# Attention scores and side work as column quarters: 64x32 tiles in place of 64x128

## The reference

```python
x = x + 0.5 * ffn(layernorm(x), k0, k1, k2, s0, s1, s2)
x = x + attn(layernorm(x), wq, bq, wk, bk, wv, bv, wo, bo)   # 16 heads of 16 dims
x = x + 0.5 * ffn(layernorm(x), k0, k1, k2, s0, s1, s2)

# ffn: weights are +1 or -1 by a boolean; features 2*256 -> 1024 -> 1024 -> 256
h = concatenate([x, -x]); h = 2 * relu(s0 * (h @ w(k0)))
h = 2 * relu(s1 * (h @ w(k1))); return s2 * (h @ w(k2))
# attn
scores = softmax(q @ k.T / sqrt(16)); att = scores @ v; return att @ wo.T + bo
```

## Time and profile before

| | |
|---|---|
| median of 3 executions | 1523.57 us (1523.52 to 1525.18) |
| span of the profiled execution, first to last instruction | 1521.2 us |
| PE busy | 1512.4 us (99%), 12471 matmul records |
| ACT busy | 1129.3 us (74%), 8 to 9 tenths in the attention stretch |
| DVE busy | 574.2 us (38%) |
| chain of work that ended last | PE 99% |
| granted TensorE clock, mean | 0.999 |

### The profile page before, as it was taken

One profiled execution on the slowest core, in us unless ns is written; L12 is line 12 of the kernel. 1 busy time (PEld: TensorE's weight loads), 2 busy tenths in 40 slices (PEclk: granted clock), 3 DMA queues, 4 the chain that ended last, 5 costly groups with the idle time before them and its releaser, 6 DMA issues.

```text
span 1521.2 us, 31574 instructions
## 1 busy us (share of the span) xinstructions
PE 1512.4 (99%) x12471; PEld 606.1 (40%) x12471; DVE 574.2 (38%) x1298; ACT 1129.3 (74%) x1654; POOL 59.7 (4%) x65
## 2 busy tenths in 40 slices
PE   9999999999999999999999999999999999999999
PEld 5555455334334333333333334334333334334354
DVE  7645764511431243234332333242241332323462
ACT  3221222888889988898989989889988988988721
POOL 2010011001000100010100000000000000000000
PEclk9999999999999999999999999999999999999999
DMA  4122223212331231232223123111213212311110
GB/s 139 42 84 51 75 80 113 71 51 81 84 73 41 96 95 40 67 113 63 81 53 95 40 53 94 39 49 59 81 39 67 82 51 65 104 41 21 47 28 16
DMA packets 110139, 101.46 MB, mean 67 GB/s; under 512 B 55846, under 2 KB 95526, under 8 KB 109990
## 3 DMA queue, kind: packets, MB, share of 16 engines
q1 hardware_dynamic: 109158, 98.60, 23.0%
q10 hardware_dynamic: 832, 0.79, 0.2%
HBM read 61.87 MB, written 25.43 MB: 57 GB/s over the span
## 4 chain that ended last, share of the span: by engine, by line
PE 99%; DVE 0%; ACT 0%; issue 0%; POOL 0%; POOLq 0%
PE psum L888 31%; PE psum L850 30%; PE psum L872 16%; PE psum L750 12%; PE psum L762 3%; PE psum L738 3%; PE psum L769 2%; PE psum L782 1%; PE psum L688 0%; PE psum L775 0%; DVE xn L972 0%; DVE h_lo L982 0%; PE psum L710 0%; DVE x_sb L987 0%; ACT xn L911 0%
## 5 line engine op out<-in xcount | busy, mean ns | idle before, releaser
L942 ACT ACTIVATE prob<-psum 128x512 f32<-128x512 f32 (+1 forms) x1438 | 1016.6, 784 | 120.1 <-PE psum L872 115.4
L888 PE MATMUL psum<-prob,v_sb 128*17 128x512 f32 x4096 | 489.4, 595 | 0.0
L872 PE MATMUL psum<-q_st,k_st 64*128 64x512 f16 x2048 | 350.1, 379 | 0.2
L915 ACT ACTIVATE h_hi<-psum 128x512 f16<-128x512 f32 x183 | 109.6, 604 | 215.8 <-PE psum L750 164.6
L980 DVE TENSOR_SCALAR h_hi<-psum 128x512 f16<-128x512 f32 x73 | 50.5, 692 | 433.8 <-PE psum L850 433.8
L982 DVE SCALAR_TENSOR_TENSOR h_lo<-psum,h_hi 128x512 f16<-128x512 f32 x256 | 169.0, 688 | 86.9 <-ACT h_hi L915 84.4
L888 PEld LDWEIGHTS psum<-prob,v_sb 128*17 128x17 f32 x4096 | 95.3, 96 | 262.9 <-issue 166.4
L872 PEld LDWEIGHTS psum<-q_st,k_st 64*128 64x128 f16 x2048 | 82.5, 94 | 279.1 <-ACT prob L942 210.7
L850 PE MATMUL psum<-h_hi,w 64*128 64x512 f16 x1184 | 152.1, 376 | 0.2 <-ACT h_hi L915 0.2
L850 PE MATMUL psum<-h_lo,w 64*128 64x512 f16 x1184 | 152.0, 376 | 0.0
L750 PE MATMUL psum<-h_hi,w 128*128 128x512 f16 x432 | 102.5, 380 | 2.2 <-DVE h_lo L982 2.2
(11 more groups left out here) (109 smaller groups left out, 860.0 us busy)
## 6 DMA issues: line engine op xcount, KB each, us to landing
k_st<-k_halves SPq DMA_DIRECT2D x64, 512.0 KB, 4.4
q_halves<-piece SPq DMA_DIRECT2D x32, 256.0 KB, 2.5
q_st<-q_halves SPq DMA_DIRECT2D x64, 128.0 KB, 4.8
x_rows<-x_sb SPq DMA_DIRECT2D x16, 256.0 KB, 2.2
k_halves<-piece SPq DMA_DIRECT2D x16, 256.0 KB, 2.8
att_rows<-o_sb SPq DMA_DIRECT2D x128, 32.0 KB
x_sb<-x_rows SPq DMA_DIRECT2D x8, 512.0 KB, 4.0
att_t<-att_rows SPq DMA_DIRECT2D x16, 256.0 KB
```

Of the source, the lines that this page charges most:

```text
L872: mm = pe.matmul(psum[:, score_bank[h + r], :], k_st[rows, slot, t * P:(t + 1) * P], q_st[rows, slot, :], start=True, stop=True)
L888: mm = pe.matmul(psum[32 * j:32 * j + va, O_BANK, :], v_sb[:, b * key_tiles + t, GROUP * g4 + j, :], prob[:, h % PROBS, :], start=(t == 0) ...
L915: act.activation(hi, psum[:, bank, :], ACT.Relu).then_inc(act_done, 1)
L942: act.activation(prob[:, to:to + count, :], psum[:, bank:bank + count, :], ACT.Exp, scale=score_scale / QK_SCALE ** 2).then_inc(exp_sem, 1)
```

## The change

Every matmul of `pe_pair` and `pe_scores` becomes four, one for each quarter of its 128 columns: the quarter's 32 columns of the weights, the same moving operand, and the quarter's 32 partitions of the same bank. A pair of two matmuls of 64 rows by 128 columns becomes a group of eight of 64 rows by 32 columns: four quarters on one half of the rows, then four on the other. The semaphore is raised by the last quarter. Waits, banks, the list of steps and the instructions of all other engines stay as they are; only line numbers move. The products with v (line 888, now 893) stay at 128 rows by 32 columns.

```diff
+        QUARTERS = [slice(c, c + P // 4) for c in range(0, P, P // 4)]
+
         def pe_pair(s):
...
                 for bank, first in ((s, 0), (s.mate, 1)):
                     r, m = (first + turned + part) % 2, bank.m
                     rows, cols = slice(64 * r, 64 * r + 64), slice(m * P, (m + 1) * P)
-                    to = psum[:, bank.bank, :]
+                    wide = slice(0, BANK)
...
-                        to = psum[:, bank.bank, column * dim:(column + 1) * dim]
+                        wide = slice(column * dim, (column + 1) * dim)
                         w, a = src[rows, k, tile * P:(tile + 1) * P], wide_w[rows, k, :]
-                    mm = pe.matmul(to, w, a, start=(turned == 0 and j == 0), stop=(turned == 1 and j == length - 1))
+                    for c in QUARTERS:
+                        mm = pe.matmul(psum[c, bank.bank, wide], w[:, c], a,
+                                       start=(turned == 0 and j == 0), stop=(turned == 1 and j == length - 1))
                     if i == 2 * n - 1:
                         mm.then_inc(mm_done, 1)
...
             for r in range(2):
                 rows = slice(64 * r, 64 * r + 64)
-                mm = pe.matmul(psum[:, score_bank[h + r], :], k_st[rows, slot, t * P:(t + 1) * P], q_st[rows, slot, :],
-                               start=True, stop=True)
+                for c in QUARTERS:
+                    mm = pe.matmul(psum[c, score_bank[h + r], :], k_st[rows, slot, t * P:(t + 1) * P][:, c],
+                                   q_st[rows, slot, :], start=True, stop=True)
             mm.then_inc(qk_sem, 1)
```

## The result

The changed kernel takes 1609.84 us (median of 4 executions, 1606.12 to 1619.18) against 1523.57 before: a ratio of 1.0568, 95% interval 1.0551 to 1.0585. The forecast was 1528.7 with a range of 1475 to 1535. The direction was right, the size was not: 86 us were lost where 5 were expected.

The account below looks back on a forecast made before the run. PE, busy 99% of the span, was taken to bound the kernel. Span 1521.2 plus 5.1 for the lag of eight starts, other terms 0, gave 1526.3; with the median 2.4 above, 1528.7 us, range 1475 to 1535.

Parts of the forecast that it names:

- More instructions: On PE, 19,900 more matmuls and as many loads; the sequencer can issue one in 0.0068 us, so cost 0.
- rival 4: PE's instruction pages come late: 167 more, 1729 us if each is exposed, 1595 if a third; chance 0.05.
- Eight starts in place of two: Ahead of the v products, the group's last matmul starts 0.02 us later a step, costing 5.1 us in all.
- The shape change: Between scores and v products, changing rows alone still costs the 0.09 to 0.10 us gap; saving 0, bounds 0 and 49.
- Rival 1: The gap at the v products goes when columns agree, saving 49 us: 1475 us; chance 0.18.
- Four streams, loads: In PE's groups, four quarters' operand streams run at full rate and loads hide under running matmuls; each costs 0.
- rivals 2 and 3: On PE: starts or streams have a floor, 1591 to about 2260 us, chance 0.08; loads come late, about 1832, chance 0.05.
- Other engines: Outside PE nothing moves; exponentials start 0.02 us later with the scores, and ACT has room.
- The sum: Whole kernel: profiled span 1521.2 + 5.1 = 1526.3; the median stands 2.4 above its span, giving 1528.7 us.

Follow-up runs that it names:

- experiments 2: Changed kernel, but from the third group of heads on only 128 of 2048 columns of k are fetched: 1573.55 us, ratio 1.0340 against the kernel before.
- 3: Changed kernel with the next group's k sent in four parts, one a step over four steps, same bytes: 1576.39 us, ratio 1.0351 against the kernel before.
- 5: Changed kernel with each transfer of k followed by an equal one into device memory nobody reads: 1670.56 us, ratio 1.0952 against the kernel before.
- the two controls: Kernel before with each k transfer doubled: 1525.10 us, ratio 1.0004; kernel before with k cut to 128 columns from the third group: 1523.64 us, ratio 0.9997.
- 1: The change with column halves, 64 columns a tile, in place of quarters: 1529.16 us, ratio 1.0036 against the kernel before.
- Experiment 4: Changed kernel with the l3 work left as pairs of 64 rows by 128 columns, quarters elsewhere: 1572.27 us, ratio 1.0322 against the kernel before.
- after_small_k: The kernel of experiments 2: the change with k cut to 128 columns from the third group of heads on, 1573.55 us.
- run 64: Not a follow-up kernel: the stretch of 64 l3 matmuls in a row in the changed kernel's own trace, which takes 0.87 us.
- double-k run: The changed kernel with each transfer of k followed by an equal one into unused device memory: 1670.56 us, ratio 1.0952.

## Why the prediction was wrong, step by step

**The step that failed: pages, in "More instructions ... Cost 0" and in rival 4.** The part on instructions asked only whether PE's sequencer can issue one in 0.0068 us. It can, but it must have it first. Rival 4 did count the pages (167 more forecast, 155 came) and how often one is due ("one every 4.8 us of attention"), and then took the packet's own 1.2 us for the price of a page and wrote "Fetched ahead, as now, it is hidden", with a chance of 0.05. Two things were wrong. The time to compare with is not the packet's own: at the waits PE goes on 2.2 to 3.0 us after a packet's start, and the packet starts 1.2 us after PE has begun the page before at the median, 5.8 us at the worst, behind a group's k and q, in transfers of 512 KB that take 5.4 us to land. That is some 3.6 us as a rule and up to 8.5 (at 1140.47), against the 3.3 and 5.2 us that a page lasts. And "as now" held for a page every 13 us: the kernel before fetched 83 between 300 and 1400 us, so it had cover for all of this; the changed one fetched 231 between 300 and 1500, one every 5.2 us with the waits counted. The rival's own version with a third of the pages exposed, 1595, was nearest to the truth: 49 late steps for 155 added pages, at 86.9 / 49 = 1.8 us each and not 1.2. That is luck, as no row stood behind its third. The rival's sign, idle stretches of about a microsecond at regular counts of instructions, is what the trace shows: 57.0 / 44 = 1.3 us, at multiples of 256.

What shows the cause: at equal instructions the loss moves with the data beside the pages (experiments 2, 3 and 5, with nothing moved in the two controls), and at equal data with the instructions in a stretch (1 and 4). The waits stand at multiples of 256 instructions, and each ends behind a page's packet. That a page is asked for about one page ahead is worked out from the packets' times, not recorded. The 21 l3 steps that stay late without the k bursts fit this too: in the dense part of an l3 step a page lasts 2.2 us, less than the 1.2 + 2.4 us that a page needs at the median from the start of the page before. In `after_small_k` the l3 wait that ends at 819.30 had next to nothing else on the DMA engines: 1.4 us to the packet and 2.5 from there. No run took all other transfers away, so how much of the 33.1 us is left to them is open.

The Trainium skill, "Runtime: NRT & Kernel Launch", section "Instruction fetch mechanics", says that instructions come in blocks of 256 while the block before is executed, and that crossing into the next is mostly hidden because an engine issues more slowly than blocks arrive. The first half agrees with this trace: 256 instructions in a packet, and waits at multiples of 256. The second does not hold for this kernel: 57.0 us of waits, on the engine that bounds it.

**Eight starts in place of two: right.** Forecast 0.02 us a step; the median step is 0.019 longer. From the last score group's first start to its last it is 23 ns at the median of undisturbed steps (3 before), and from that last start to the first v product 306 ns in both kernels. All steps that are not late sum to 6.8 us against 5.1.

**The shape change: right, no gain.** 306 - 216 = 0.09 us, the same whether rows alone change or both. Rival 1 (1475 us) needed less than 0.07. Experiment 4 measured the third kind, columns alone at 64 rows: 0.09 to 0.12 at each of four places.

**Four streams, loads: right.** Groups of eight take 0.216 us, in l3 (656.24 - 655.37) / 8 = 0.109, the numbers of the prediction, over runs of 64 matmuls: 0.87 / 64 = 0.0136 us a start. That ends rivals 2 and 3. The Trainium skill's 25 ns as the least distance between matmul starts ("TensorE: Matmul & The Clock Gate", section "Wait — 56ns, not 53.3ns?"), which the prediction cited against the change, would by an estimate from that figure have made this run 64 x 0.025 = 1.6 us; the trace, with 0.87, does not agree.

**Other engines: right.** Busy times of DVE, ACT and POOL moved by less than 5 us.

**The sum.** Its 2.4 us are the median less the span of another execution. Within one execution they are 4.0 (1525.18 against 1521.2; 4.1 in the changed kernel). The forecast does not hang on it, as it comes to the median before plus 5.1 us.

## What to carry to other kernels

Cutting a matmul into column tiles multiplies instructions at equal work: count how long 256 of them last on the engine at its densest place, and compare that with how long a page takes to arrive, counted from the start of the page before (here some 3.6 us at the median, up to 8.5 behind the longest burst of data), not with what an instruction costs to issue. Where an engine stops at "issue" in the middle of work that has no wait, look in the DMA view for the instruction packet that ends it, and count whether the stops stand at equal distances in instructions. Long transfers cut into portions spread over steps let pages through; an instruction saved in the densest stretch does too, if it brings no new change of tile shape at 0.1 us each.

## What was not expected of the hardware

- Around some of the long waits the granted clock falls. Windows of the changed kernel around the wait at 658.7 (stretch, its us, then busy us and instructions under way: PE, PEld, DVE, ACT, POOL; granted clock, DMA share, GB/s):

```profile
658.00:660.00 2.00, 0.72 (x8) 0.10 (x1) 0.00 (x0) 1.36 (x2) 0.00 (x0) 1.00 0.77 290
660.00:662.00 2.00, 0.00 (x0) 0.00 (x0) 0.00 (x0) 0.00 (x0) 0.00 (x0) 0.76 0.04 10
662.00:664.00 2.00, 1.51 (x8) 0.15 (x7) 0.00 (x0) 0.00 (x0) 0.00 (x0) 0.50 0.04 8
664.00:666.00 2.00, 2.00 (x52) 0.98 (x56) 0.69 (x1) 0.97 (x2) 0.00 (x0) 0.50 0.00 1
666.00:668.00 2.00, 2.00 (x88) 1.44 (x72) 0.00 (x0) 0.54 (x1) 0.00 (x0) 0.54 0.23 51
668.00:670.00 2.00, 2.00 (x68) 0.81 (x52) 1.33 (x2) 1.98 (x3) 0.00 (x0) 1.00 0.12 26
```

  PE had stood still since 658.71. The clock went to 0.50, the level of 1.2 GHz, and was back at 1.00 from 668 on: the 64 l3 matmuls at 665.16 take 666.87 - 665.16 = 1.71 us, beside 0.87 at 655.37. This happened at four places of the attention stretch, at the waits that end at 349.65, 662.49, 975.77 and 1268.65. It did not happen at two others that are as long, which end at 502.22 and 1140.47, 3.6 and 3.5 us after the matmul start before (2.5 at 349.65). The windows at the four places (two microseconds each, times one less the granted clock) sum to 10 us, so part of the 86.9 us in late steps is a second bill for the same waits. In the double-k run it is 26 us, in the run with spread transfers none.
- In 64-column tiles a load takes 107 ns, beside 93 for 32 columns, and the first two score groups of a step take 14 ns more than with 32 or 128 (456 ns, beside 442). That is most of what the halves cost; the quarters pay about as much in lag.
